# h built row by row: an add and a max in one instruction, on GpSimd and ScalarE

## What is computed

```python
hi = x @ W1[:H]                                   # one row a_i for each node i
hj = x @ W1[H:]                                   # one row b_j for each node j
h  = relu(hi[:, None, :] + hj[None, :, :] + b1)   # 128 x 128 x 128: every pair of nodes
y  = layernorm(h @ W2 + b2) * gamma + beta        # every pair again
x1 = layernorm(x + einsum('ij,ijh->ih', adj, y))
# then an attention layer over x1, with adj as a weight of exp(s), and a last layernorm
```

## Time and profile before

| | before |
|---|---|
| time, median of 3 runs | 2622.48 us (2622.45 to 2622.6) |
| span of the profiled execution | 2621.4 us |
| PE busy | 2577.0 us (98%) |
| DVE busy | 2337.8 us (89%) |
| ACT busy | 2332.6 us (89%) |
| POOL busy | 1999.1 us (76%) |
| mean granted TensorE clock | 0.998 of full speed |

### The profile page before, as it was taken

The page is one execution under the profiler, slowest core; times in us unless marked ns, Lnnn a source line. Parts: engine busy times, 40 slices in busy tenths (PEclk is TensorE's granted clock), DMA queues, the critical chain, the costliest instruction groups (busy, mean ns, idle before and its releaser), DMA issues.

```text
span 2621.4 us, 77145 instructions
## 1 busy us (share of the span) xinstructions
PE 2577.0 (98%) x21263; PEld 2049.5 (78%) x21263; DVE 2337.8 (89%) x18135; ACT 2332.6 (89%) x3650; POOL 1999.1 (76%) x1163
## 2 busy tenths in 40 slices
PE   8999999999999999999999999999999999999997
PEld 7777777777777777777777777777777777777774
DVE  7889988989899889998898989988988999989897
ACT  7899899899998998989989889999899898998996
POOL 7777777777777777777777777777777777777773
PEclk9999999999999999999999999999999999999999
DMA  0000000000000000000000000000000000000000
GB/s 17 8 12 7 11 7 10 11 6 11 11 6 11 6 11 11 6 11 11 6 11 6 11 11 6 11 10 7 11 6 11 11 6 11 8 8 11 6 7 7
DMA packets 48051, 23.49 MB, mean 9 GB/s; under 512 B 6208, under 2 KB 47808, under 8 KB 47808
## 3 DMA queue, kind: packets, MB, share of 16 engines
q1 hardware_dynamic: 46512, 21.12, 2.9%
q10 hardware_dynamic: 1296, 0.20, 0.0%
HBM read 17.11 MB, written 4.19 MB: 8 GB/s over the span
## 4 chain that ended last, share of the span: by engine, by line
PE 58%; DVE 24%; issue 11%; ACT 6%; POOL 0%; ACTq 0%; DVEq 0%; DMA 0%
PE y_ps L529 42%; DVE squares L517 16%; PE agg_ps L573 12%; DVE q L517 3%; ACT y L263 3%; DVE x1e L488 2%; ACT h L281 1%; ACT L334 1%; PE prep_ps L529 1%; PE tail_ps L529 1%; DVE o_sb L455 1%; PE tail_ps L584 1%; PE att_ps L529 1%; DVE eT L509 0%; DVE si_cols L499 0%
## 5 line engine op out<-in xcount | busy, mean ns | idle before, releaser
L252 POOL TENSOR_TENSOR h<-bT,aT 128x1024 f32<-128x1024 f32 x1024 | 1951.1, 1919 | 584.3 <-PE y_ps L529 572.9
L529 PEld LDWEIGHTS y_ps<-w_pair,h 128*128 128x128 f32 x16384 | 1885.7, 192 | 313.0 <-DVE q L517 260.3
L529 PE MATMUL y_ps<-w_pair,h 128*128 128x128 f32 x16384 | 1991.3, 278 | 21.9 <-DVE q L517 9.3
L517 DVE CUSTOM_DVE_ANT_0 squares<-y_ps,y 128x128 bf16<-128x128 f32 x8192 | 1842.3, 282 | 185.0 <-ACT y L263 171.2
L263 ACT ACTIVATE y<-y_ps 128x508 f32<-128x508 f32 x2048 | 1162.4, 595 | 190.8 <-PE y_ps L529 173.9
L281 ACT ACTIVATE h<-h 128x1024 f32<-128x1024 f32 x1024 | 1085.3, 1060 | 10.2 <-POOL h L252 10.2
L517 DVE DVE_READ_ACCUMULATOR2_ANT q<- 128x1 f32 x8192 | 659.1, 80 | 0.0
L573 PE MATMUL agg_ps<-y,wz 128*32 128x512 f32 x4096 | 545.9, 606 | 1.7 <-DVE o_sb L455 1.7
L573 PEld LDWEIGHTS agg_ps<-y,wz 128*32 128x32 f32 x4096 | 81.1, 108 | 66.7 <-issue 3.1
L492 DVE CUSTOM_DVE_ANT_0 s_terms<-x1e,v1row 128x128 f32<-128x128 f32 x64 | 99.5, 1554 | 0.1
L334 ACT ACT_TABLE_LOAD x64 | 82.1, 1283 | 4.3 <-DVE sj L504 3.2
(11 more groups left out here) (90 smaller groups left out, 740.4 us busy)
## 6 DMA issues: line engine op xcount, KB each, us to landing
x_in<-in_x_dram SPq DMA_DIRECT2D x64, 64.0 KB, 1.8
adj_in<-in_adj_dram SPq DMA_DIRECT2D x64, 64.0 KB, 1.9
x_res<-in_x_dram SPq DMA_DIRECT2D x64, 64.0 KB, 1.8
adj_res<-in_adj_dram SPq DMA_DIRECT2D x64, 64.0 KB, 1.9
out_dram<-x_out SPq DMA_DIRECT2D x64, 64.0 KB, 1.6
w<-in_L_gnn_W_dram ACTq DMA_DIRECT2D x1, 64.0 KB, 2.4
w1a<-in_L_gnn_W_dram SPq DMA_DIRECT2D x1, 64.0 KB, 2.2
w1b<-in_L_gnn_W_dram SPq DMA_DIRECT2D x1, 64.0 KB, 2.3
```

What stands on the lines that cost most here:

```text
L252: nc.gpsimd.tensor_tensor(h[:, u % HRING].rearrange("k (r g) s -> k r g s", g=GROUPS), bT[:, p, :].unsqueeze(1).unsqueeze(1).broadcast_to( ...
L517: last = nc.vector.tensor_tensor_reduce(out=squares[:, k % YRING, n, :], in0=y_ps[k % YRING][:, n, :], in1=y[:, p, i, :], scale=1.0, scala ...
L529: return nc.tensor.matmul(dst, lhsT, rhs, start=start, stop=stop)
```

## The change

Each of the 8 rows of a unit is now made by an instruction of its own, which adds the column of a to b and takes the maximum with zero. Rows 0 to 6 are TENSOR_SCALAR on POOL, 128x128 each; row 7 is an ACTIVATE Relu on ACT with the column of a as bias. The 1024-wide add and the 1024-wide relu are gone. PE waits for both makers, and ACT's row waits for nothing of POOL; like POOL it waits until PE has read unit u-4 out of the ring.

```diff
+    POOL_ROWS = 7
...
+        def row(u, n):
+            return n % GROUPS * GROUP + u * QPU + n // GROUPS
...
                         pool.wait_ge(y_in_psum, t * QUARTS + (u - HRING + 1) * QPU)
-                    shape = [K, QPU, GROUPS, S]
-                    a_now = aT[:, p, :].rearrange("k (g r) -> k r g", g=GROUPS)[:, u * QPU:(u + 1) * QPU, :]
-                    nc.gpsimd.tensor_tensor(
-                        h[:, u % HRING].rearrange("k (r g) s -> k r g s", g=GROUPS),
-                        bT[:, p, :].unsqueeze(1).unsqueeze(1).broadcast_to(shape),
-                        a_now.unsqueeze(3).broadcast_to(shape), ALU.add).then_inc(u_ready, 1)
+                    pool.sem_inc(pool_passed, 1)
+                    for n in range(POOL_ROWS):
+                        i = row(u, n)
+                        last = nc.gpsimd.tensor_scalar(h[:, u % HRING, n, :], bT[:, p, :], aT[:, p, i:i + 1], 0.0, ALU.add, ALU.max)
+                    last.then_inc(h_pool, 1)
...
-            def relu(t, u):
-
-                act.wait_ge(u_ready, t * UNITS + u + 1)
-                nc.scalar.activation(h[:, u % HRING], h[:, u % HRING], ACT.Relu).then_inc(h_ready, 1)
+            def act_rows(t, p, u, first):
+
+                if u == 0:
+                    act.wait_ge(ab_sb_s, t + 1)
+                if not (first and u < HRING):
+                    act.wait_ge(y_in_psum, t * QUARTS + (u - HRING + 1) * QPU)
+                for n in range(POOL_ROWS, UNIT):
+                    i = row(u, n)
+                    last = nc.scalar.activation(h[:, u % HRING, n, :], bT[:, p, :], ACT.Relu, bias=aT[:, p, i:i + 1])
+                last.then_inc(h_act, 1)
...
                     if pairs:
 
-                        pe.wait_ge(h_ready, t * UNITS + u + 1)
+                        pe.wait_ge(h_pool, t * UNITS + u + 1)
+                        pe.wait_ge(h_act, t * UNITS + u + 1)
```

More of the change, by code:

```diff
@@ L135, in gnn_pair_kernel @@
         ab_ps_s, ab_sb_s = sem("ab_in_psum"), sem("ab_in_sbuf")
-        u_ready, h_ready = sem("preact_ready"), sem("h_ready")
+        h_pool, h_act = sem("h_rows_from_pool"), sem("h_rows_from_act")
         y_in_psum, y_stored, q_done = sem("y_in_psum"), sem("y_stored"), sem("q_done")
@@ L145, in gnn_pair_kernel @@
             sem(n) for n in ("adj_sum_ready", "x_beta_ready", "sj_ready", "si_sum_ready", "si_ready"))
-        s_passed = sem("statistics_wait_passed")
+        s_passed, pool_passed = sem("statistics_wait_passed"), sem("pool_row_wait_passed")
         out_ready = sem("out_ready")
@@ L295, in _ @@
             for u in range(2):
-                relu(0, u)
+                act_rows(0, 0, u, True)
             def slot(t, half, p, pairs, prep, gather, tail, finish, early):
@@ L337, in slot @@
                         if ahead < UNITS:
-                            relu(t, ahead)
+                            act_rows(t, p, ahead, early == 0)
                         elif prep:
-                            relu(t + 1, ahead - UNITS)
+                            act_rows(t + 1, 1 - p, ahead - UNITS, False)
                         for k in range(u * QPU, (u + 1) * QPU):
@@ L479, in slot @@
                         if early >= 1:
-                            dve.wait_ge(u_ready, t * UNITS)
+                            dve.wait_ge(h_pool, t * UNITS)
+                            dve.wait_ge(h_act, t * UNITS)
                         project(t + 1, 1 - p)
```

## The result

| | before | with the change |
|---|---|---|
| time, median | 2622.51 us | 5051.7 us (5050.16 to 5054.32) |
| ratio | | 1.926, 95% interval 1.9235 to 1.929 |
| span of the profiled execution | 2621.4 us | 5048.1 us (its own time 5050.16) |
| a slot | 40.23 and 40.59 us | 78.2 us on average |
| mean granted TensorE clock | 0.998 | 0.839 |

What follows compares the result with a forecast made beforehand. PE was taken as the bound, with 59 us of stalls from late DVE. Slots of 39.55 us, 0.86 less, times 61 give -52 us, plus 3 for the first slot: about 2574 us, range 2550 to 2645.

Steps and rivals of the forecast that it cites:

- POOL's price: Time of one 128x128 TENSOR_SCALAR on POOL, taken as COPY's 0.292 us: 2.04 us a unit, 33.5 us a slot, under PE.
- The slower rival: POOL becomes the bound: fetching the column adds 0.087 us, 0.379 us an instruction, about 2815 us in all; chance 0.22.
- the upper bound: POOL's dearest 128x128 instruction, a TENSOR_TENSOR at 0.526 us, taken as the most a TENSOR_SCALAR could cost: 59.7 us a slot.
- the break-even view: POOL decides the time from 0.345 us an instruction; from 0.354 us the kernel is slower than before.
- PE's stalls: PE's waits for late DVE, 0.96 us a slot over 61 slots: 59 us, 2.2%, the most any saving could give.
- units 12 and 13 lose their 0.45 us: PE's stalls at units 12, 13 and transpose L595, from DVE waiting for POOL's adds: 0.45 us gone in both slots.
- PE's second wait: PE's additional wait for h, made by POOL and ACT: claimed to cost nothing, both parts being done units ahead.
- L488 and L492: Two DVE instructions of 0.98 and 1.59 us that waited for POOL's adds; each was to fall to near 0.4 us.
- First, the Exp: First cause of DVE's lateness: ACT's relu behind the Exp delays the copy of y; DVE was to start 0.68 us earlier.
- The stall of units 4 and 5: PE taking 4.19 us and not 3.77 there, 0.42 us lost, put down to DVE's lag from the Exp.
- The 0.27 us behind the turn: PE's loss behind agg_ps after the loop's turn, 1.26 us against 0.99, put down to DVE's lag from the Exp.
- The rival "no change": Short POOL instructions follow without a gap, so DVE waits as long as before: 2617 to 2628 us; chance 0.07.

Runs made afterwards that it cites:

- the 84 ns of that run: The changed kernel, with POOL's seven TENSOR_SCALAR of a unit adding the constant 0.5 in place of the column of a: 4437.4 us, 0.604 us an instruction.
- the run with three rows: The changed kernel with 3 rows of a unit on POOL, one on ACT and four left out as zero: 2585.6 us, ratio 0.9859.
- the cut in two: The kernel before, with POOL's add of 1024 cut into two of 512: 2609.84 us, ratio 0.995.
- the cut in four: The kernel before with DVE's o_sb steps half a unit later and POOL's add in four of 256: 2609.81 us, ratio 0.9951.
- the run with both edits: The kernel before, with POOL's add in two of 512 and DVE's o_sb steps half a unit later: 2586.46 us, ratio 0.9863.

## Why the prediction was wrong, point by point

**The step that failed is POOL's price**, "I take COPY's, since both stream one tensor in and one out": 0.292 us was taken, 0.688 measured. What failed was more than the choice. I called a MEMSET and a TENSOR_TENSOR bounds of a TENSOR_SCALAR because they have the same shape, and the true price lay above the dearer one. Nothing in the trace said that price goes by the streams; for this instruction 0.435 of the 0.688 us goes by the element, 3.40 ns each, and 0.110 is its second arithmetic step, quantities no POOL row of the trace before had. The slower rival failed by the same step: its own addition, the column, was right to 3 ns (0.087 against 0.084), on a base that was wrong, and by luck, since it took for one column the difference between a COPY of 128 elements and a MEMSET. The Trainium skill, GPSIMD Engine Reference, "Performance pitfalls for Q7 kernels", gives some 102 cycles for a small read, by my estimate 85 ns, and the 84 ns of that run agree in size; that the column is such a read isn't shown.

**The range failed by a second step.** The text worked out that at the upper bound a slot is 59.7 us, called it ruinous, and gave it no chance; the range ended where POOL was just the bound. An unknown that decides from 0.354 us on, with a stated bound of 0.526, should have carried its upper end into the range or been the reason for a wide one. The way from price to time was right: with 0.688 in place of 0.292 the prediction's own line, 112 x price + 0.82, gives 77.9 us a slot against 78.2 measured, and 61 x (78.2 - 40.4) = 2306 of the 2427 us that the span grew. The first slot needed 108 us more until its first L584 counterpart (210.49 against 102.65), which is nearly all of the rest.

**What held:** the break-even view, that POOL decides from 0.345 to 0.354 us on; that all there was to gain is PE's stalls (PE's own work 39.45 predicted, 39.4 in the run with three rows); ACT's row (0.37 predicted, 0.393 measured); that units 12 and 13 lose their 0.45 us once the wait for the port is gone; that PE's second wait and the added semaphore cost nothing to be seen.

**Right by luck:** L488 and L492 near 0.4 us (0.382 and 0.362 measured). The prediction got there with half of a 0.3 us POOL instruction to wait. POOL's instructions are 0.69 us and follow each other without a gap, so by the same reckoning x1e would have taken some 0.35 + 0.34 = 0.69 us. What failed is the step "Instructions that met the port now wait for at most one POOL instruction": DVE doesn't wait for the end of POOL's TENSOR_SCALAR (x1e 0.343 us in the median, 0.59 at most).

**What was wrong beside the price:** "First, the Exp". Moving the relu away from behind the Exp changed nothing, twice, since eT or v then waited for POOL's add. The stall of units 4 and 5 is the distance from agg_ps over o_sb to the bank, shown by the run that moved o_sb. So even with a cheap POOL instruction the change would not have reached 2574: the run with three rows, in which POOL is no bound, takes 2585.6. The 0.27 us behind the turn went in that run, where DVE came to the turn 0.74 us sooner and v no longer waited for POOL (0.29 us long at most turns); the two were not told apart.

**The rival "no change"** (short POOL instructions leave DVE no gap) was no part of this result: L498 took 0.343 us in the median beside POOL's unbroken TENSOR_SCALARs. That doesn't show DVE slipping in between, as the prediction argued, but that there is no lock. Where POOL's short instructions are TENSOR_TENSORs, the rival is real, as the last section shows.

## What to carry to other kernels

A shape doesn't price an instruction on GpSimd: if the operation itself isn't in the trace, its cost is open upwards, and one run that times 28 of them back to back is worth more than any bound from its neighbours. Ask first what an engine's busy time is worth: here 59 us of PE's stalls were all that 2000 us of POOL and 1085 us of relu could ever give back, against a loss without limit. For waits for the port that VectorE and GpSimd share, look in the trace at where VectorE's instruction starts in GpSimd's and where it ends: here the cut in two gained 13 us and 36 with VectorE's order settled for it, and the cut in four gave 23 of them back.

## What was unexpected in the hardware

On POOL, TENSOR_SCALAR with an add and a max costs 0.253 us and 3.40 ns an element, TENSOR_TENSOR 0.138 us and 1.70 ns. One arithmetic step less in TENSOR_SCALAR saves 0.110 us on 128 elements; whether all of that goes by the element wasn't measured.

Whether POOL locks DVE out depends on POOL's operation: its TENSOR_TENSOR does, its TENSOR_SCALAR of one tensor and a column doesn't, though both read SBUF (x1e inside a single TENSOR_SCALAR in 62 of 64 cases with three rows on POOL, inside an add in none).

A DVE instruction that needs the port may be passed over again and again. In the run with rows by TENSOR_TENSOR, x1e took 4.51 us in the mean:

```profile
1448.82 5.74 POOL L257 TENSOR_TENSOR h<-bT,aT 128x128 f32<-128x128 f32 x16
...
1449.56 4.72 DVE L498 TENSOR_SCALAR x1e<-x1p,mv,rs 128x128 f32<-128x128 f32 x1
```

It ends at 1454.28, when the last of the 16 runs; POOL then stood, since PE in its turn had waited for DVE ("2.43 <-DVE q" in the row of PE). This fits slots of 44 us, where 0.356 us an instruction, about the break-even, would give 40.7; no run takes this wait away alone. The same shows with 256 elements, above, and not with TENSOR_SCALAR on POOL, nor with adds of 512 or 1024, where DVE got in at the end of the add in which it started, or, where it started 0.02 us before the next add, at the end of that one (x_beta in the run with both edits, 1.22 us). The Trainium skill, SBUF — State Buffer, "Who interferes with whom", says that the loser is blocked for the other's whole instruction; here it was blocked for 13 of them, and beside TENSOR_SCALAR for none. What decides whether DVE gets in between two adds stays open.

TensorE's granted clock was 0.839 in the mean with the change, so it changed between its two levels, 2.4 and 1.2 GHz, in a slot in which PE again and again waited for POOL (1.00 from 2487 to 2497 us, 0.61 from 2547 to 2556, where PE was busy 1.90 of 8.90 us); before, PE was never long idle and the clock 0.998. The mean agg_ps took 756 ns and not 606. It cost nothing here, as PE waited anyway.
